# Splitting the expert weights, rows and inner values of two feed-forward stages into rounded high parts and rests

## The chip, the cores and the metric

The kernel runs on one core of one Trainium2 chip. The core has a matrix engine (PE, TensorE), whose weight loads are listed as PEld, a vector engine (DVE), a scalar engine (ACT), a general engine (POOL, GpSimd) and a queue of DMA instructions (SP). The metric is the device time of one execution in microseconds (us). Below, "pitch" is the distance between the starts of two neighbouring instructions of one kind.

## The reference, cut to what matters

A small network of eight stages in float32: an attention and a feed-forward stage in turn, each added to `x` after a normalisation. The change touches the feed-forward stages. The first two of them, called gated here, compute this on 1024 rows of 256 values:

```python
shared = _silu_and_mul(x @ shared_gate_up_w.T) @ shared_down_w.T      # inner width 704
shared = shared * jax.nn.sigmoid(x @ shared_gate_w.T)
probs = jax.nn.softmax(x @ gate_w.T, axis=-1)
routing_weights, selected_experts = jax.lax.top_k(probs, 2)           # 8 experts
for e in range(8):
    w_e = jnp.where(selected_experts == e, routing_weights, 0.0).sum(-1)
    h = _silu_and_mul(x @ w13[e].T) @ w2[e].T                         # inner width 176
    combined = combined + w_e[:, None] * h
out = shared + combined
```

The last two feed-forward stages (late) have the same experts' part, a smaller shared part (inner width 176) and no sigmoid.

## The kernel before, in words

One function, `ffn_stage`, writes each feed-forward stage as five programs, one for an engine, that run beside each other and wait for each other's semaphores. Within an engine the order is the order of the code. `early` is true in the two gated stages, where the shared part is cut in six pieces, four of them (`n_first`) ahead of the experts.

A gated stage runs in three parts. In the **front**, the 1024 rows are normalised and turned, the router's logits come out of PE, and DVE works out the routing in a chain of small instructions (lines 686 to 754): softmax, the two best experts of each row (`hit`), a rank from PE (`rank`, which waits for `hits_done`), and from it the lists `from_row` and `to_row` that say which rows make up each of 23 tiles of 128 rows (`rows_known`), and which expert owns a tile (`owner`). Meanwhile PE multiplies the first shared pieces: in its order stand `up(0, 0)`, `rank`, `up(0, 1)`, `up(1, 0)`, the list products, `up(1, 1)`, `clear_acc`, and `down(0)`, which waits for both `h_low(0, ...)` of DVE. ACT takes the gate products through `silu` and rounds `h` to a high part `h_hi`; DVE subtracts to get the rest `h_lo`. After `rows_known` PE has the rest of the first four pieces to do, and POOL starts eight gathers of 128 rows each (line 349).

In the **expert loop** each tile goes PE `turn_x` (L471, transpose of the gathered rows), ACT `x_out` (L610), PE `expert_up` (L484, two products of 128x352), ACT `silu_of` (L616) and DVE `h_of_tile` (L829), PE `turn_h` (L495), ACT `h_out` (L622), PE `expert_down` (L508, two products of 88x256), ACT `y_out` (L628), POOL `scatter` (L356). The tiles overlap: in PE's order `turn_x(i + 3)`, `expert_up(i + 2)`, `expert_down(i)` and `turn_h(i + 1)` follow each other. POOL alternates a scatter with a gather for the tile eight ahead (`XG_RING`), for 15 of the 23 tiles, and then only scatters. `y` has four buffers (`Y_RING`). These products take plain float32. The shared pieces use `product` (L78 to L80) instead: operands are split in a rounded high part and a rest of type fp32r, and high x high, rest x high and high x rest are added up.

In the **tail** the last two shared pieces and the scattered rows are added.

The eight experts' weights (128x1216 each, 608 KB) are loaded by SP in one go in the front and used as they come. POOL does nothing in the front between the store of the normalised rows and the first gather.

## Time and profile before

| | |
|---|---|
| median of 3 runs | 1727.43 us (1725.33 to 1733.93) |
| profiled execution, its own time | 1732.21 us |
| its span | 1730.4 us |
| busy: PE, DVE, ACT, POOL | 85%, 53%, 44%, 24% |
| granted PE clock, mean | 0.94 of full |

The profiled execution is one run with its own time; the span runs from its first instruction to its last. Line numbers are those of the kernel before. A "busy" share is an average over all eight stages. In the rows, one plain float32 product appears as two PE records, and names of tiles are written without their stage and number. A note in square brackets at the end of a row is how long the engine had been idle before it and what it waited for. In rows of a stretch, each engine has its busy time with the number of its instructions, then come the granted PE clock, the DMA share and GB/s.

### The profile page before, as it was taken

Reading aid. Unit: us, or ns where it says so; the run is one execution under the profiler, and the core shown is the slowest. Engines: PE = TensorE matmul, PEld = TensorE weight load, DVE = VectorE, ACT = ScalarE, POOL = GpSimd, SP = SyncE. Lnnn points to the kernel's source line nnn. Section 1 sums busy time; section 2 is a strip of 40 time slices with the busy share of each in tenths; the row PEclk is TensorE's granted clock in tenths of the full one; section 3 lists DMA queues with packets and bytes.
Section 4 is the critical chain, followed back from the end, with each engine's and each line's share of the span. In section 5 each row is a group of like instructions: output and inputs, shape, how many; then the busy total and the mean of one; then the engine's idle time right before and its main releaser. Section 6 shows DMA issues by size and latency. Waiting matters only on the chain. (4 is left out here: it accounts for less than half of the span.)

```text
span 1730.4 us, 27960 instructions
## 1 busy us (share of the span) xinstructions
PE 1476.0 (85%) x10106; PEld 1110.5 (64%) x10112; DVE 912.3 (53%) x1968; ACT 754.0 (44%) x1872; POOL 411.3 (24%) x328
## 2 busy tenths in 40 slices
PE   6999999995799789999899879878887787898587
PEld 4777787874576667767676657665555566533466
DVE  5766665663731846565555563176554314376712
ACT  5565656561334333433434434433443342586242
POOL 2607061210235221110201014520000451100162
PEclk9999999997899899999999989988897898899699
DMA  4002020100612400010000051230003223000423
GB/s 145 29 13 80 2 92 2 55 2 20 227 52 78 143 13 31 0 42 0 12 30 1 1 206 55 77 103 1 1 1 137 94 77 99 1 1 1 180 87 116
DMA packets 42996, 99.88 MB, mean 58 GB/s; under 512 B 7168, under 2 KB 21760, under 8 KB 42752
## 3 DMA queue, kind: packets, MB, share of 16 engines
q1 hardware_dynamic: 32736, 69.85, 11.8%
q0 software_dynamic: 9984, 28.32, 5.0%
q8 instruction: 76, 1.25, 0.3%
q14 instruction: 40, 0.33, 0.1%
q10 hardware_dynamic: 160, 0.13, 0.0%
HBM read 79.93 MB, written 18.35 MB: 57 GB/s over the span
## 5 line engine op out<-in xcount | busy, mean ns | idle before, releaser
L829 DVE TENSOR_TENSOR s_h_e<-s_bank,s_silu_e 128x176 f32<-128x176 f32 x92 | 31.4, 341 | 221.9 <-ACT s_silu_e L616 209.7
L484 PE MATMUL s_bank<-s_expert_w,s_xe 128*128 x368 | 130.5, 479 | 0.8 <-ACT s_xe L610 0.7
L508 PE MATMUL s_bank<-s_expert_w,s_he 88*128 x368 | 97.7, 387 | 30.6 <-ACT s_he L622 30.6
L356 POOL DMA_INDIRECT expert_rows<-s_y,s_to_row x92 | 91.3, 992 | 126.2 <-ACT s_y L628 114.3
L124 POOL TENSOR_SCALAR ln_var<-ln_moments 128x4 f32<-128x4 f32 x16 | 4.2, 260 | 492.3 <-DVE ln_moments L117 369.4
L349 POOL DMA_INDIRECT s_xg<-normed_rows,s_from_row x92 | 92.2, 1002 | 119.9 <-DVE s_from_row L744 93.1
L508 PEld LDWEIGHTS s_bank<-s_expert_w,s_he 88*128 88x128 f32 x368 | 68.4, 191 | 62.3 <-issue 43.7
L2555 POOL TENSOR_TENSOR s_w_hi<-s_w_raw,zero 128x1024 fp32r<-128x1024 f32 x25 | 55.3, 2213 | 220.6 <-PE s_memory L80 188.0
L1160 ACT ACTIVATE s_scratch<-s_bank,s_neg_max 128x128 f32<-128x128 f32 (+3 forms) x128 | 67.2, 528 | 89.2 <-DVE s_neg_max L1250 89.2
L1250 DVE TENSOR_REDUCE s_neg_max<-s_bank 128x1 f32<-128x128 f32 (+3 forms) x128 | 59.7, 488 | 74.2 <-PE s_bank L1063 74.1
L1080 PE MATMUL s_bank<-s_probs_t,s_v 128*128 128x512 f32 (+3 forms) x256 | 76.3, 441 | 20.2 <-ACT s_probs_t L1168 20.2
L1061 PE MATMUL s_bank<-s_k,s_q 128*128 128x128 f32 (+3 forms) x256 | 90.0, 447 | 3.0 <-ACT s_scratch L1160 2.2
L78 PE MATMUL s_bank<-xn_t_hi,s_w_hi 128*128 128x512 f32 x192 | 85.6, 446 | 7.8 <-DVE s_earlier L683 5.3
L981 POOL TENSOR_TENSOR s_w_hi<-s_w_raw,zero 128x1024 fp32r<-128x1024 f32 x11 | 22.3, 2026 | 272.1 <-PE s_bank L80 123.0
L2222 ACT ACTIVATE s_exps<-s_bank,s_rms 128x512 f32<-128x512 f32 x128 | 76.7, 696 | 21.3 <-PE s_bank L2108 21.3
L1080 PEld LDWEIGHTS s_bank<-s_probs_t,s_v 128*128 128x128 f32 x256 | 46.5, 190 | 55.0 <-ACT s_probs_t L1168 25.7
L484 PEld LDWEIGHTS s_bank<-s_expert_w,s_xe 128*128 128x128 f32 x368 | 65.3, 198 | 22.9 <-issue 4.3
L79 PE MATMUL s_bank<-xn_t_lo,s_w_hi 128*128 128x512 f32 x192 | 78.9, 411 | 0.0
L80 PE MATMUL s_bank<-xn_t_hi,s_w_lo 128*128 128x512 f32 x192 | 78.7, 410 | 0.0
L628 ACT ACTIVATE s_y<-s_bank 128x256 f32<-128x256 f32 x92 | 35.3, 384 | 94.0 <-PE s_bank L508 46.6
L1168 ACT ACTIVATE s_probs_t<-s_bank 128x128 f32<-128x128 f32 (+3 forms) x128 | 49.0, 437 | 59.9 <-PE s_bank L1074 59.9
L1260 DVE TENSOR_SCALAR s_scratch<-s_scratch,s_row_sum 128x128 f32<-128x128 f32 (+3 forms) x128 | 68.7, 537 | 4.5
(386 smaller groups left out, 4294.7 us busy)
## 6 DMA issues: line engine op xcount, KB each, us to landing
s_expert_w<-in_experts SPq DMA_DIRECT2D x32, 608.0 KB, 12.9
s_w_raw<-in_wa_o SPq DMA_DIRECT2D x16, 512.0 KB, 4.2
s_yg<-expert_rows SPq DMA_DIRECT2D x32, 256.0 KB, 4.6
s_raw<-in_shared SPq DMA_DIRECT2D x16, 384.0 KB, 6.9
normed_rows<-s_ln_xn POOLq DMA_DIRECT2D x8, 512.0 KB, 9.5
s_w_raw<-in_wa_k SPq DMA_DIRECT2D x4, 512.0 KB, 3.9
s_w_raw<-in_wa_v SPq DMA_DIRECT2D x4, 512.0 KB, 3.5
s_w_raw<-in_wa_q SPq DMA_DIRECT2D x4, 512.0 KB, 4.9
```

The source lines that it names most:

```text
L78: pe.matmul(out, sh, mh, start=first, stop=False, skip_group_check=True)
L79: pe.matmul(out, sh, ml, start=False, stop=False, skip_group_check=True)
L80: return pe.matmul(out, sl, mh, start=False, stop=last, skip_group_check=True)
L349: pool.indirect_dma_start(out=xg[:, i % XG_RING, :], out_offset=None, in_=x_rows[:, :], in_offset=bass.IndirectOffsetOnAxis(ap=from_row[:, ...
L356: pool.indirect_dma_start(out=y_rows[:, :], out_offset=bass.IndirectOffsetOnAxis(ap=to_row[:, i:i + 1].bitcast(U32), axis=0), in_=y[:, i % ...
L484: last = pe.matmul(u_bank[i % 2][:, 0:2 * INTER], xe[:, i % 2, x], expert_of(P, i, w), start=c == 0, stop=c == DC - 1, skip_group_check=True)
L508: last = pe.matmul(y_bank[i % 2][:, 0:D], he[0:IHALF, i % 2, h], expert_of(IHALF, i, w), start=c == 0, stop=c == 1, skip_group_check=True)
L1061: pe.matmul(to, q[:, b, h * S + r * P:h * S + (r + 1) * P], k[:, b, h, 0:(r + 1) * P], start=r == UNIT_ROWS[u][0], stop=False, skip_group_ ...
L1080: last = pe.matmul(o_bank[:, j * P:S], v[:, b, j, h * DH:(h + 1) * DH], probs_t[:, j, j * P:S], start=j == 0, stop=j == TB - 1, skip_group ...
L1160: act.activation(probs[:, h % 2, r, 0:(r + 1) * P], score_bank(h, r), ACT.Exp, bias=neg_max[:, 4 * h + r:4 * h + r + 1], accum_out=row_sum ...
L1260: dve.tensor_scalar(mine, mine, one, None, ALU.mult).then_inc(probs_done, 1)
L2222: act.activation(exps[:, s % 2, g, :], s_bank[g][:], ACT.Exp, scale=rms[:, b, 1, j:j + 1]).then_inc(exp_done, 1)
```

## The change

In the gated stages the experts' products are made like the shared ones, from split operands.

- Weights: `e_raw` holds three experts' raw weights (in the memory of `yg`, not needed until the tail). ACT rounds each expert to `e_hi` (128x1216, `expert_high`), and POOL subtracts to get `e_lo` (eight times, ahead of its waits for `x_stored` and `rows_known` and of the gathers). SP loads expert 3 and later ones into a slot when `e_lo` of the slot's last expert is done. ACT's eight copies stand at three places: three right after `gate_exp`, three after both `silu` of shared piece 0, two after those of piece 1.
- Rows and inner values: `x_out` and `h_out` write rounded tiles `xe_hi` and `he_hi`; DVE gets two more instructions for a tile, `x_low` (128x256) and `h_low_of_tile` (88x256), both PSUM tile minus SBUF tile.
- Products: three fp32r products in place of each plain one. PE waits for all eight `e_lo` ahead of the loop.
- `Y_RING` goes from 4 to 6, in all four feed-forward stages. The late stages have no other change.
- Memory: in the gated stages `silu` and `h_full` share memory with the normalised rows (so ACT waits for `x_stored` before its first `silu`), `logits_t` lies in `xg` and `slot_hit` in `y`.

```diff
-XG_RING, Y_RING = 8, 4
+XG_RING, Y_RING = 8, 6
+E_RING = 3
...
+            def expert_raw(one):
+                if one >= E_RING:
+                    sp.wait_ge(e_lo_done, one - E_RING + 1)
+                sp.dma_start(e_raw[:, one % E_RING, :], experts[one]).then_inc(e_raw_loaded[one % E_RING], 16)
...
                 sp.dma_start(raw[:, n % 3, :], shared[n]).then_inc(raw_loaded[n % 3], 16)
+                if early and n in (2, 3):
+                    for one in range(E_RING) if n == 2 else range(E_RING, N_EXP):
+                        expert_raw(one)
...
+            if early:
+                for one in range(N_EXP):
+                    pool.wait_ge(e_hi_done, one + 1)
+                    pool.tensor_tensor(e_lo[:, one, :], e_raw[:, one % E_RING, :], f32(e_hi[:, one, :]),
+                                       ALU.subtract).then_inc(e_lo_done, 1)
             pool.wait_ge(x_stored, 16 * NHALF)
             pool.wait_ge(rows_known, 1)
...
-                    last = pe.matmul(u_bank[i % 2][:, 0:2 * INTER], xe[:, i % 2, x], expert_of(P, i, w),
-                                     start=c == 0, stop=c == DC - 1, skip_group_check=True)
+                        last = product(pe, u_bank[i % 2][:, 0:2 * INTER], (xe_hi[:, i % 2, x], xe_lo[:, i % 2, x]),
+                                       (expert_of(e_hi, P, i, w), expert_of(e_lo, P, i, w)), c == 0, c == DC - 1)
...
+            def expert_high(one):
+                act.wait_ge(e_raw_loaded[one % E_RING], 16 * (one // E_RING) + 16)
+                act.activation(e_hi[:, one, :], e_raw[:, one % E_RING, :], ACT.Copy).then_inc(e_hi_done, 1)
+
+            if early:
+                for one in range(3):
+                    expert_high(one)
+                act.wait_ge(x_stored, 16 * NHALF)
...
                                        ACT.Silu).then_inc(silu_done, 1)
+                    if early and n < 2:
+                        for one in ((3, 4, 5), (6, 7))[n]:
+                            expert_high(one)
...
+            def x_low(i):
+                dve.wait_ge(xe_hi_done, i + 1)
+                if i >= 2:
+                    dve.wait_ge(u_ready, i - 1)
+                dve.tensor_tensor(xe_lo[:, i % 2, :], xt_bank[i % 2][:, 0:D], f32(xe_hi[:, i % 2, :]),
+                                  ALU.subtract).then_inc(xe_done, 1)
...
             if early:
-                for b in range(4):
-                    add_shared(b, 1)
-            for i in range(TILES):
-                h_of_tile(i)
+                add_shared(0, 1)
+                x_low(0)
+                x_low(1)
+                add_shared(1, 1)
+                add_shared(2, 1)
+                h_of_tile(0)
+                x_low(2)
+                add_shared(3, 1)
+                h_of_tile(1)
+                h_low_of_tile(0)
+                for i in range(TILES):
+                    if i + 3 < TILES:
+                        x_low(i + 3)
+                    if i + 2 < TILES:
+                        h_of_tile(i + 2)
+                    if i + 1 < TILES:
+                        h_low_of_tile(i + 1)
```

The order of POOL's instructions in the first gated stage (`s1`), around the store of the normalised rows, before:

```order
L127 TENSOR_TENSOR ln_rstd<-ln_var,ln_power 128x4
L343 DMA normed_rows<-s1_ln_xn 128x4x256 x2
L349 DMA s1_xg<-normed_rows,s1_from_row 128x256 x8
L356 DMA expert_rows<-s1_y,s1_to_row 4992x256
L349 DMA s1_xg<-normed_rows,s1_from_row 128x256
```

and now (`s1_yg` holds the raw weights):

```order
L128 TENSOR_TENSOR ln_rstd<-ln_var,ln_power 128x4
L367 DMA normed_rows<-s1_work 128x4x256 x2
L387 TENSOR_TENSOR s1_expert_lo<-s1_yg,s1_expert_hi 128x1216 x8
L373 DMA s1_xg<-normed_rows,s1_from_row 128x256 x8
L380 DMA expert_rows<-s1_y,s1_to_row 4992x256
```

Eight subtractions now stand between the store and the first gather; the rest of the order is the same.

ACT's order in the same stage from `gate_exp` on, before:

```order
L585 ACTIVATE s1_gate_exp<-s1_logits 128x8
L593 ACT_TABLE_LOAD
L593 ACTIVATE s1_silu<-s1_bank4 128x512
L593 ACTIVATE s1_silu<-s1_bank6 128x512
L599 ACTIVATE s1_h_hi<-s1_h_full 128x512 x2
L593 ACTIVATE s1_silu<-s1_bank4 128x512
L593 ACTIVATE s1_silu<-s1_bank6 128x512
L599 ACTIVATE s1_h_hi<-s1_h_full 128x512 x2
L570 ACTIVATE s1_w_hi<-s1_raw 128x768
```

and now (`s1_work` holds `silu` and `h_full`):

```order
L625 ACTIVATE s1_gate_exp<-s1_logits 128x8
L629 ACTIVATE s1_expert_hi<-s1_yg 128x1216 x3
L642 ACT_TABLE_LOAD
L642 ACTIVATE s1_work<-s1_bank4 128x512
L642 ACTIVATE s1_work<-s1_bank6 128x512
L629 ACTIVATE s1_expert_hi<-s1_yg 128x1216 x3
L651 ACTIVATE s1_h_hi<-s1_work 128x512 x2
L642 ACTIVATE s1_work<-s1_bank4 128x512
L642 ACTIVATE s1_work<-s1_bank6 128x512
L629 ACTIVATE s1_expert_hi<-s1_yg 128x1216 x2
L651 ACTIVATE s1_h_hi<-s1_work 128x512 x2
```

Three copies came ahead of the first `silu`, three ahead of the two roundings of `h` for piece 0, and two ahead of those for piece 1.

PE's order for one tile of the expert loop, from `turn_x` over `find_owner` (the load and two register instructions) to the first product of `expert_up`, before:

```order
L471 MATMUL s1_bank7<-ident,s1_xg 128x128 x2
L515 TENSOR_LOAD s1_owner
L515 ISA x2
L484 ISA
L484 MATMUL s1_bank5<-s1_expert_w,s1_xe 128x352
```

and now, over the same stretch:

```order
L500 MATMUL s1_bank7<-ident,s1_xg 128x128 x2
L552 TENSOR_LOAD s1_owner
L552 ISA x2
L79 ISA
L79 MATMUL s1_bank5<-s1_expert_hi,s1_xe_hi 128x352
L80 REGISTER_ALU
L80 MATMUL s1_bank5<-s1_expert_lo,s1_xe_hi 128x352
L81 MATMUL s1_bank5<-s1_expert_hi,s1_xe_lo 128x352
```

Where one plain product stood with one register instruction ahead, three rounded ones stand with two. The same holds for the second product of `expert_up` and for both of `expert_down`.

## Rows read from the trace of the kernel before

**Rows 1.** Windows: PE, PEld, DVE, ACT, POOL busy us (instructions), clock, DMA share, GB/s.
```profile
452.00:468.40 16.40, 14.31 (x74) 10.92 (x76) 13.12 (x61) 4.97 (x9) 0.00 (x0) 0.90 0.60 243
468.40:491.50 23.10, 23.10 (x148) 20.74 (x148) 12.81 (x24) 8.47 (x13) 8.71 (x8) 1.00 0.16 46
```

**Rows 2.** Timeline of ACT, front of the first gated stage (start, duration, work, idle before).
```profile
452.83 0.20 ACT L585 ACTIVATE s_gate_exp<-s_logits 128x8 f32<-128x8 f32 x1
458.52 0.60 ACT L593 ACTIVATE s_silu<-s_bank 128x512 f32<-128x512 f32 x1 [3.58 <-PE s_bank L80]
```

**Rows 3.** Timeline of DVE, same stretch: routing chain.
```profile
456.32 0.22 DVE L706 TENSOR_TENSOR s_hits<-s_hit 128x64 bf16<-128x64 f32 x1
461.54 2.36 DVE L732 TENSOR_TENSOR s_slot_hit<-s_routing,s_in_slot 128x1024 bf16<-128x1024 f32 x2
467.90 0.18 DVE L744 TENSOR_SCALAR s_from_row<-s_to_row 128x23 int32<-128x23 int32 x1
```

**Rows 4.** Timeline of POOL and DVE in the second attention stage.
```profile
649.33 1.89 POOL L981 TENSOR_TENSOR s_w_hi<-s_w_raw,zero 128x1024 fp32r<-128x1024 f32 x1 [31.68 <-DMA s_w_raw<-in_wb_k]
649.48 1.90 DVE L1260 TENSOR_SCALAR s_scratch<-s_scratch,s_row_sum 128x256 f32<-128x256 f32 x1
651.30 2.38 POOL L984 TENSOR_TENSOR s_w_lo<-s_w_raw,s_w_hi 128x1024 fp32r<-128x1024 f32 x1
651.48 2.42 DVE L1260 TENSOR_SCALAR s_scratch<-s_scratch,s_row_sum 128x384 f32<-128x384 f32 x1
```

**Rows 5.** Timeline of POOL and DVE in the first attention stage.
```profile
59.58 2.41 POOL L2558 TENSOR_TENSOR s_w_lo<-s_w_raw,s_w_hi 128x1024 fp32r<-128x1024 f32 x1
59.81 2.72 DVE L2915 SCALAR_TENSOR_TENSOR s_sigma_qt<-s_exp_part,s_positive 128x512 f32<-128x512 f32 x1 [1.46 <-ACT s_positive L2820]
```

**Rows 6.** Timeline of POOL and DVE, second attention stage, an earlier place.
```profile
597.49 3.34 POOL L981 TENSOR_TENSOR s_w_hi<-s_w_raw,zero 128x1024 fp32r<-128x1024 f32 x1 [11.23 <-DMA s_w_raw<-in_wb_v]
598.99 1.87 DVE L1227 TENSOR_SCALAR s_bq<-s_bq 128x16 f32<-128x16 f32 x1
```

**Rows 7.** Line 2558: the POOL subtraction of two SBUF tiles (min/median/max ns).
```profile
L2558 POOL TENSOR_TENSOR s_w_lo<-s_w_raw,s_w_hi x25: 2355/2407/2730, 39.8 to 352.0; 128x1024 fp32r<-128x1024 f32 x25
```

**Rows 8.** Line 570: an ACT copy that rounds SBUF to SBUF.
```profile
L570 ACT ACTIVATE s_w_hi<-s_raw x16: 833/842/864, 446.0 to 1621.0; 128x768 fp32r<-128x768 f32 x16
```

**Rows 9.** The page's part 6: a weight load (KB each, us to landing).
```profile
s_w_raw<-in_wa_o SPq DMA_DIRECT2D x16, 512.0 KB, 4.2
```

**Rows 10.** Timeline of PE: rounded products of 256 columns.
```profile
470.07 0.28 PE L78 MATMUL s_bank<-s_w_hi,s_h_hi 128*128 128x256 f32 x1
470.19 0.28 PE L79 MATMUL s_bank<-s_w_lo,s_h_hi 128*128 128x256 f32 x1
```

**Rows 11.** Timeline of PE in the expert loop: the two transposes of a tile.
```profile
509.19 0.38 PE L495 MATMUL s_bank<-ident,s_h_e 128*88 128x128 f32 x2
509.41 0.38 PE L471 MATMUL s_bank<-ident,s_xg 128*128 128x128 f32 x2
```

**Rows 12.** Timeline of ACT, line 628 alone: the copies y_out of the expert loop.
```profile
498.08 0.39 ACT L628 ACTIVATE s_y<-s_bank 128x256 f32<-128x256 f32 x1 [0.55 <-PE s_bank L508]
500.57 0.38 ACT L628 ACTIVATE s_y<-s_bank 128x256 f32<-128x256 f32 x1 [0.55 <-PE s_bank L508]
507.44 0.38 ACT L628 ACTIVATE s_y<-s_bank 128x256 f32<-128x256 f32 x1 [1.88 <-remote]
559.77 0.38 ACT L628 ACTIVATE s_y<-s_bank 128x256 f32<-128x256 f32 x1 [1.30 <-PE s_bank L508]
```

**Rows 13.** Timeline of POOL in that loop: a scatter.
```profile
510.67 1.00 POOL L356 DMA_INDIRECT expert_rows<-s_y,s_to_row  x1 [0.30 <-issue]
```

**Rows 14.** Line 628: what ended one kind of its waits (us, times).
```profile
  remote: 42.0, 17
```

**Rows 15.** Windows around an idle PE ahead of a late feed-forward stage.
```profile
1320.00:1325.50 5.50, 0.06 (x1) 0.06 (x1) 4.30 (x14) 0.00 (x0) 1.34 (x2) 0.50 0.09 26
1328.00:1331.00 3.00, 2.26 (x9) 1.70 (x8) 2.94 (x7) 2.59 (x5) 0.09 (x1) 0.50 0.90 307
```

More of the change, by code:

```diff
@@ L226, in ffn_stage @@
         xt_bank, u_bank, ht_bank, y_bank = (banks[4], banks[7]), banks[5:7], banks[0:2], banks[2:4]
-        norm = Norm(nc, ctx, sem, f"{name}_ln", res, [b[:] for b in banks[4:8]], measured=measured)
+        work = sb("work", [P, 2 * NHALF, HALF])
+        silu, h_full = work[:, 0:NHALF, :], work[:, NHALF:2 * NHALF, :]
+        norm = Norm(nc, ctx, sem, f"{name}_ln", res, [b[:] for b in banks[4:8]], measured=measured,
+                    xn=work[:].rearrange("p a (b d) -> p (a b) d", d=D) if early else None)
         following = Moments(sem, "next_ln", res)
@@ L231, in ffn_stage @@
         w_hi, w_lo = sb("w_hi", [P, 3, SH_COLS], F32R), sb("w_lo", [P, 3, SH_COLS], F32R)
-        e = sb("expert_w", [P, N_EXP, EXP_COLS])
+        yg = sb("yg", [P, TOP_K, NT, D])
+        y = sb("y", [P, Y_RING, D])
+        if early:
+            e_hi, e_lo = sb("expert_hi", [P, N_EXP, EXP_COLS], F32R), sb("expert_lo", [P, N_EXP, EXP_COLS], F32R)
+            e_raw = yg[:].rearrange("p k t d -> p (k t d)")[:, 0:E_RING * EXP_COLS].rearrange("p (r n) -> p r n", r=E_RING)
+        else:
+            e = sb("expert_w", [P, N_EXP, EXP_COLS])
         tables = sb("routing", [P, TABLE_COLS])
@@ L291, in ffn_stage @@
         xt_ready, xe_done, e_loaded = sem("xt_ready"), sem("xe_done"), sem("expert_w_loaded")
+        e_raw_loaded = [sem(f"expert_raw_loaded{r}") for r in range(E_RING)]
+        e_hi_done, e_lo_done = sem("expert_hi_done"), sem("expert_lo_done")
+        xe_hi_done, he_hi_done = sem("xe_hi_done"), sem("he_hi_done")
         u_ready, silu_e_done, h_e_done = sem("u_ready"), sem("silu_e_done"), sem("h_e_done")
@@ L507, in expert_down @@
                     w = slice(EXP_DOWN + c * D, EXP_DOWN + (c + 1) * D)
-                    last = pe.matmul(y_bank[i % 2][:, 0:D], he[0:IHALF, i % 2, h], expert_of(IHALF, i, w),
-                                     start=c == 0, stop=c == 1, skip_group_check=True)
+                    if early:
+                        last = product(pe, y_bank[i % 2][:, 0:D], (he_hi[0:IHALF, i % 2, h], he_lo[0:IHALF, i % 2, h]),
+                                       (expert_of(e_hi, IHALF, i, w), expert_of(e_lo, IHALF, i, w)), c == 0, c == 1)
+                    else:
+                        last = pe.matmul(y_bank[i % 2][:, 0:D], he[0:IHALF, i % 2, h], expert_of(e, IHALF, i, w),
+                                         start=c == 0, stop=c == 1, skip_group_check=True)
                 last.then_inc(y_ready, 1)
```

48 lines of the change are left out of this document (35 added, 13 removed).

## The prediction

> **What bounds the kernel now.** I read the page first, then the busy time of the engines in windows of a gated stage, then the timelines of the engines in them, and last two places elsewhere where POOL does what it is now to do in the front.
>
> In the front of the first gated stage PE is busy 14.31 of 16.40 us and DVE 13.12, while POOL has not one instruction [rows 1]. After it comes a stretch of 23.10 us in which PE has no gap at all [rows 1]. So whatever moves the end of the front moves everything behind it by as much; and that end is the end of DVE's routing chain. It runs without a break from the hits at 456.32 over the slot comparison at 461.54 to `from_row`, which ends at 468.08 [rows 3]. The second gated stage has the same code and sizes; I give it the same.
>
> In the expert loop two tiles without a stall are 2.49 us apart, yet the 22 intervals from 498.08 to 559.77 take 61.69 us where 22 x 2.49 would be 54.8 [rows 12]. The rest are stalls: the first three tiles take 9.36 us instead of 7.47, and the wait that ends it is given as "remote" [rows 12], which stands for 17 waits and 42.0 us over all four feed-forward stages [rows 14].
>
> **The loop: products.** Per tile, four plain products become twelve rounded ones. The rounded product of 256 columns has a pitch of 0.12 us [rows 10]. The trace has none of 352 columns; in proportion to the columns it takes 0.162. Six of 0.162 and six of 0.118 are 1.68 us, and the two pairs of transposes keep 0.22 each [rows 11]: 2.12 us of PE work in place of 2.49. That is the lower end of the new period. The upper end is the old 2.49: the path from `turn_h` over `h_out` to `expert_down` gets one more instruction, `h_low_of_tile`, and PE's queue has twice the register instructions for a tile. I take 2.30, the middle.
>
> The Trainium skill ("TensorE: Matmul & The Clock Gate", Back-to-back issue gap and the section on 56 ns ahead of it) gives an isolated matmul of N columns N/2.4 + 2.5 ns; for 352 that is 149 ns and for 256 it is 109. The trace is 8% above that at 256 columns. By the page the PE work would be 1.99 us a tile and not 2.12; what the runs show per tile decides.
>
> **The loop: stalls.** They are no lack of `y` buffers. The copy that stalls at 507.44 is that of tile 3 (498.08, 500.57, one more, then this), the first use of the fourth buffer, which waits for no store at all [rows 12]. What it waits for is PE's signal, which arrives late while POOL is issuing a gather. So the ring of six cures nothing by itself, and the two late stages, which get only that, stay as they are (0 us; bound: rival C). In the gated stages the stalls depend on how PE's signals fall against POOL's issues. POOL needs 1.30 us for a scatter [rows 13] and as much for a gather, 2.6 a tile for the first 15 tiles, so at a period of 2.30 the two drift apart and a signal meets an issue now and then. I take three stalls of 1.9 us (from 9.36 - 7.47), with none and seven as ends. Loop: 22 x 2.30 + 5.7 = 56.3, that is -5.4 us a stage; -11.1 without stalls, about -1 with a period near 2.4 and all stalls kept. POOL's 15 x 2.6 + 8 x 1.3 = 49 us stay below that.
>
> Between front and loop DVE has to make two or three `x_low` ahead of the first up product: +0.3 us.
>
> **The front: ACT.** Eight copies of 128x1216. A rounding copy of 128x768 takes 0.84 us [rows 8]; in proportion to the columns less some fixed part I estimate 1.22, or 9.8 us in all. ACT has 4.97 of 16.40 us busy there [rows 1], so its time is there; its order is what costs. The first three end at 456.7 and hold back the first `silu`, which had nothing but a table load ahead of it; its result is needed by `h_of(0, 0)`, which costs the chain up to 2. Experts 3 to 5 can only be loaded when `e_lo` of 0 to 2 is done: with 2.86 us each for those (below) the last is done at 462.9, a load takes some 4.3 us (512 KB take 4.2 [rows 9]), the copy 1.2, so `h_hi` of piece 0, which stands behind it in ACT's order, comes at 468.4 and not right behind the `silu` of 458.52 [rows 2]. `h_low(0, 0)` stands in DVE's order ahead of the last six routing instructions. That alone puts `rows_known` at 471.2 in place of 468.1: **+3.1 us**.
>
> **The front: POOL beside DVE.** This is the main term. The subtraction on POOL takes 2.36 to 2.73 us for 128x1024 [rows 7]; for 128x1216 I estimate 2.86 from the median 2.41, and eight are 23 us. While such an instruction runs, certain DVE instructions do not get through: a 128x256 multiplication by a scalar takes 1.90 us and ends 0.16 after POOL's; the next one takes 2.42 and again ends 0.22 after POOL's next, which had slipped in between [rows 4]. The 128x512 one with two SBUF inputs takes 2.72 and ends 0.55 after POOL's [rows 5], and even one of 128x16 takes 1.87 and ends with it [rows 6]. So with POOL's instructions back to back, DVE gets one such instruction done per POOL instruction.
>
> The routing chain is made of these: comparisons, products and casts of SBUF tiles. Walking both queues forward: `e_hi(0)` is done at 454.3 (`gate_exp` ends at 453.03 [rows 2] plus 1.2), POOL runs `e_lo(0)`, (1), (2) until 463.5 with handovers of 0.2. DVE reaches its cast of the indices 0.6 ahead of the hits, at 455.7, gets it done at 457.3, the first comparison at 460.2, the second and the sum `hits` at 463.7 instead of 456.54: +7.2. PE's `rank` waits for it, and behind `rank` PE's gate product for `silu(0, 1)`, which was ready at 458.52 [rows 2], 2.0 after the hits; ACT's next copies stand behind that `silu`. So POOL pauses until about 468, DVE runs free for that time up to the tile comparisons, and then `e_lo(3)`, (4) and (5) each hold one of the large comparisons or the `h_low`: three more blocks of 2.6 to 2.9, 8.2 us. Then ACT's queue needs `h_of(0, 1)`, POOL is idle and the rest runs free. Sum +15.4 a stage, `rows_known` at 483.5; the 3.1 us of ACT's order lie inside it. Low end: if casts and scalar instructions on integers do not block, 13.1. High end: four blocks in the second group, 18.4. `e_lo(6)` and (7) and the gathers follow under the 23.1 us of PE work and cost nothing; were that cover gone, 5.7 us.
>
> The Trainium skill ("SBUF — State Buffer", Who interferes with whom) says that a DVE instruction with two SBUF inputs contends with a GpSimd instruction that reads SBUF, that copies, casts and `tensor_scalar` contend only in a two-port mode, that reductions never do, and that whoever issues first holds the shared ports for the whole instruction. The trace agrees on the first, with 2.72 us of which 0.55 lay behind POOL's end, and shows a scalar instruction of 128x16 blocked too (1.87 us, where one of 128x23 in the chain takes 0.18 [rows 3]). If the small casts are not in that mode, the front would be the low end, 13.1.
>
> **The clock.** PE will wait some 10 us in the front. After an idle stretch of 5.50 us elsewhere it is still granted half speed (0.50, 1.2 GHz) in a window 2.5 to 5.5 us later [rows 15]. If the first 3 to 7 us of the 23.10 run at half speed, that costs half of them; I take 2.0, ends 0 and 3.3.
>
> **Sum.** Per gated stage +15.4 + 2.0 + 0.3 - 5.4 = +12.3, rounded to 12; two are +24. The profiled execution took 1732.21 us and would take 1756; it lies 4.8 above the median of its runs, 1727.43, and the forecast on that is 1751. Own range: low 13.1 + 0 + 0.3 - 11.1 = +2.3 a stage (1732), high 18.4 + 3.3 + 0.3 - 1 = +21 (1769).
>
> **Rivals.** A: the front is not blocked. The rows on blocking are of instructions on large tiles or alone in a queue, and the chain has other semaphores between its steps, which might let several instructions through at each handover. Then a stage costs +3.1 + 0.3 - 5.4 = -2.0, total 1723; with no stalls 22 x 2.30 gives -7.7, total 1712. The point from which it decides: the front and the clock together must grow by under 9.4 us a stage for the whole to stay within 8.6 us of before. For it speaks nothing in the trace that I found; against it, rows 4 to 6. C: the ring of six is what the "remote" waits wanted. Then all 17 go, 1.9 us each: -32 over four stages; with the blocked front 1727 + 2 x (15.4 + 2.0 + 0.3 - 11.1) - 17 of the late stages = about 1724, and without it near 1696. Against it speaks the stall on the fourth buffer. D: the loop gains nothing (the chain over `h_low_of_tile` or PE's queue keeps 2.49 and the stalls stay): 2 x 17.7 = +35, 1762.
>
> **Chances.** What a measurement of this kernel can tell from no change is about 0.5%, 8.6 us. Forecast 0.72 (slower 0.64, same 0.08); A 0.15 (same 0.08, faster 0.07); C 0.06 (half same, half faster); D 0.07 (slower). Together slower 0.71, same 0.19, faster 0.10. The range takes the forecast's own and reaches down into A: 1721 to 1769.
>
> **What would show it.** In the profile after: long DVE times (1 to 3 us) on lines of the routing chain that took 0.2, each ending with a POOL subtraction; POOL subtractions of about 2.9 us; `rows_known` some 15 us later against the stage's start; the stretch of unbroken PE work still 23 us or a little over. In the loop, product pitches of 0.16 and 0.12, tiles 2.3 us apart, some waits called "remote" left; the late stages unchanged to the tenth of a us. A front that grows by 3 us or less would make the main term wrong; remote waits gone from the late stages would make the reading of the ring wrong; a loop period of 2.49 would leave no gain at all.

## The result, and the profile after

The changed kernel takes 1769.09 us (median of 4 runs, 1764.86 to 1781.26), the one before 1728.35 (4 runs, 1725.33 to 1733.93): a ratio of 1.025, 95% interval 1.0219 to 1.0281. The profiled execution after took 1766.43 us with a span of 1764.6. The forecast was 1751 with a range to 1769. The time lies 0.09 us outside that edge, which decides nothing by itself (the sum behind it, 1727.43 + 2 x 21, is 1769.4); what has to be explained is that the loss of 41 us is 1.7 times the 24 forecast.

The two spans differ by 34.2 us. Read off the timelines (row maximum of the logits, `rows_known`, first and last `y_out` of each stage), in us:

| stretch | before | after | forecast |
|---|---|---|---|
| row maximum to `rows_known`, gated 1 and 2 | 15.92, 15.90 | 31.64, 31.66 | +15.4 each |
| `rows_known` to `y_out(0)`, gated 1 and 2 | 30.01, 30.04 | 32.53, 31.84 | +2.3 each |
| loop, gated 1 and 2 | 61.69, 62.00 | 64.03, 64.19 | -5.4 each |
| loop, late 1 and 2 | 62.11, 62.20 | 60.56, 60.72 | 0 |
| all the rest (difference) | | -3.1 | 0 |

The windows that answer to [rows 1]: the front, the stretch right after `rows_known`, and the rest of the PE work. Columns as there.

```profile
452.00:483.00 31.00, 14.84 (x74) 10.63 (x72) 30.17 (x54) 12.48 (x14) 24.64 (x9) 0.78 0.38 127
482.00:485.00 3.00, 3.00 (x12) 2.33 (x11) 2.80 (x8) 1.01 (x2) 2.17 (x2) 0.50 0.15 44
485.00:488.00 3.00, 3.00 (x18) 3.00 (x17) 0.95 (x2) 0.22 (x1) 2.18 (x3) 0.57 0.32 87
488.00:506.00 18.00, 18.00 (x108) 15.89 (x108) 7.31 (x11) 7.24 (x11) 3.52 (x4) 1.00 0.13 38
```

POOL, idle in the front before, is busy 24.64 of 31.00 us, DVE shows 30.17 and PE 14.84. The granted PE clock is half (0.50, 1.2 GHz) behind `rows_known`, still 0.57 on average from 485 to 488, and full (1.00, 2.4 GHz) afterwards.

The same stretch on POOL's and DVE's timelines; it answers to [rows 3]. First two rows of before that are not there, then the rows after:

```profile
455.92 0.36 DVE L704 TENSOR_TENSOR s_hit<-iota,s_at_f 128x64 f32<-128x64 f32 x2
...
467.46 0.18 DVE L742 TENSOR_TENSOR s_row<-s_row,s_spare 128x23 f32<-128x23 f32 x1
```

```profile
452.00 8.20 POOL L387 TENSOR_TENSOR s_expert_lo<-s_yg,s_expert_hi 128x1216 fp32r<-128x1216 f32 x3 [9.61 <-ACT s_expert_hi L629]
465.67 15.87 POOL L387 TENSOR_TENSOR s_expert_lo<-s_yg,s_expert_hi 128x1216 fp32r<-128x1216 f32 x5 [5.48 <-ACT s_expert_hi L629]
```

```profile
453.49 1.33 DVE L756 CAST s_at_f<-s_at 128x16 f32<-128x16 uint32 x1
454.86 5.42 DVE L758 TENSOR_TENSOR s_hit<-iota,s_at_f 128x64 f32<-128x64 f32 x2
460.31 0.23 DVE L760 TENSOR_TENSOR s_hits<-s_hit 128x64 bf16<-128x64 f32 x1
...
465.33 4.99 DVE L786 TENSOR_TENSOR s_y<-s_routing,s_in_slot 128x1024 bf16<-128x1024 f32 x2
...
470.25 0.68 DVE L718 TENSOR_TENSOR s_work<-s_bank,s_work 128x512 f32<-128x512 f32 x1
470.85 2.67 DVE L725 TENSOR_TENSOR s_h_lo<-s_work,s_h_hi 128x512 fp32r<-128x512 f32 x1
...
473.65 0.18 DVE L794 TENSOR_TENSOR s_row<-s_row,s_bank 128x23 f32<-128x23 f32 x1
...
474.08 2.08 DVE L796 TENSOR_TENSOR s_row<-s_row,s_spare 128x23 f32<-128x23 f32 x1
476.20 2.68 DVE L797 SCALAR_TENSOR_TENSOR s_to_row<-s_row,s_routing 128x23 int32<-128x23 f32 x1
478.91 2.66 DVE L798 TENSOR_SCALAR s_from_row<-s_to_row 128x23 int32<-128x23 int32 x1
```

The two comparisons of `hit` took 5.42 us where they took 0.36, the cast ahead of them 1.33 where a cast took 0.17, the two of `slot_hit` 4.99 against 2.36, and three instructions of 128x23 took 2.08, 2.68 and 2.66 against 0.18 each. Between 460.2 and 465.7 POOL paused, and there the chain runs at its old pace. Two kinds of DVE instruction were not held while POOL ran: the index searches, and those that take one of two inputs from PSUM (`s_bank`), 0.68 us at 470.25 and 0.18 us at 473.65 as before. The subtraction itself, and the copies ACT makes for it:

```profile
L387 POOL TENSOR_TENSOR s_expert_lo<-s_yg,s_expert_hi x16: 2732/2772/3782, 452.0 to 1070.8; 128x1216 fp32r<-128x1216 f32 x16
```

```profile
L629 ACT ACTIVATE s_expert_hi<-s_yg x16: 1200/1210/1217, 450.7 to 1068.7; 128x1216 fp32r<-128x1216 f32 x16
```

In the loop, the `y_out` rows that answer to [rows 12], and the sum that answers to [rows 14]:

```profile
514.10 0.38 ACT L682 ACTIVATE s_y<-s_bank 128x256 f32<-128x256 f32 x1 [0.38 <-PE s_bank L81]
...
516.39 0.38 ACT L682 ACTIVATE s_y<-s_bank 128x256 f32<-128x256 f32 x1 [0.40 <-PE s_bank L81]
...
520.49 0.38 ACT L682 ACTIVATE s_y<-s_bank 128x256 f32<-128x256 f32 x1 [1.87 <-remote]
...
522.74 0.38 ACT L682 ACTIVATE s_y<-s_bank 128x256 f32<-128x256 f32 x1 [1.12 <-PE s_bank L81]
...
526.86 0.38 ACT L682 ACTIVATE s_y<-s_bank 128x256 f32<-128x256 f32 x1 [1.89 <-remote]
```

```profile
  remote: 30.4, 15
```

Between two stalls a tile takes 2.25 to 2.29 us (forecast 2.30), but in the first two thirds of the loop about every second one stalls and takes 4.1: seven such tiles in each gated loop against five before. The profile calls ten of these fourteen waits remote, as it does seven of the ten before; the others it puts down to PE or names no releaser for. In 13 of the fourteen the copy starts 0.80 to 0.93 us behind the end of a gather; here is the one ahead of the copy at 520.49:

```profile
518.66 0.97 POOL L373 DMA_INDIRECT s_xg<-normed_rows,s_from_row  x1 [0.31 <-issue]
```

A gather being issued is not enough for a stall, though: the copy at 516.39 started inside one (516.07 to 517.05).

The products of PE in that loop, answering to [rows 10]:

```profile
530.06 0.32 PE L81 MATMUL s_bank<-s_expert_hi,s_xe_lo 128*128 x1
530.22 0.32 PE L79 MATMUL s_bank<-s_expert_hi,s_xe_hi 128*128 x1
...
530.70 0.28 PE L79 MATMUL s_bank<-s_expert_hi,s_he_hi 88*128 x1
530.83 0.28 PE L80 MATMUL s_bank<-s_expert_lo,s_he_hi 88*128 x1
```

Their pitch is 0.16 us for 352 columns and 0.12 to 0.13 for 256, as forecast.

### The profile page after: what moved, and what is told of

The parts are those of the page before. It is cut to its first block and busy times, and to the rows that moved or that the text cites. A ratio compares the mean times of both kernels' runs of the same rounds, so it can differ in the third digit from the quotient of the medians.

```text
span 1764.6 us, 28724 instructions
## 1 busy us (share of the span) xinstructions
PE 1478.1 (84%) x10296; PEld 1126.6 (64%) x10296; DVE 982.6 (56%) x2060; ACT 772.3 (44%) x1888; POOL 458.1 (26%) x344
## 5 line engine op out<-in xcount | busy, mean ns | idle before, releaser
L373 POOL DMA_INDIRECT s_xg<-normed_rows,s_from_row x92 | 90.8, 987 | 70.0 <-DVE s_from_row L798 43.2
L1878 DVE TENSOR_REDUCE s_neg_max<-s_pair 128x2 f32<-128x1024 f32 (+3 forms) x64 | 51.7, 823 | 36.3 <-PE s_pair L1656 35.5
L2999 DVE SCALAR_TENSOR_TENSOR s_sigma_qt<-s_exp_part,s_positive 128x512 f32<-128x512 f32 x32 | 50.5, 1584 | 29.9 <-ACT s_positive L2904 29.8
L517 PE MATMUL s_bank<-s_expert_w,s_xe 128*128 x184 | 64.8, 476 | 0.0
L2642 POOL TENSOR_TENSOR s_w_lo<-s_w_raw,s_w_hi 128x1024 fp32r<-128x1024 f32 x25 | 63.4, 2537 | 2.0
## 6 DMA issues: line engine op xcount, KB each, us to landing
s_expert_w<-in_experts SPq DMA_DIRECT2D x16, 608.0 KB, 11.7
```

Source lines behind the costliest of these rows:

```text
L373: pool.indirect_dma_start(out=xg[:, i % XG_RING, :], out_offset=None, in_=x_rows[:, :], in_offset=bass.IndirectOffsetOnAxis(ap=from_row[:, ...
L517: last = pe.matmul(u_bank[i % 2][:, 0:2 * INTER], xe[:, i % 2, x], expert_of(e, P, i, w), start=c == 0, stop=c == DC - 1, skip_group_check ...
L2642: pool.tensor_tensor(w_lo[:, slot, :], w_raw[:, slot, :], f32(w_hi[:, slot, :]), ALU.subtract).then_inc(w_split[slot], 1)
```

## The experiments

Four sets, each on one chip and with runs of the kernel before among them. In the first set the kernel before took 1697.5 us, in the others 1726.1, 1730.9 and 1736.6. The difference goes with the remote waits: in the loops of the first set no trace has one (the kernel before has no trace of its own there, but e1_ring6 took the same 1697.5 us). So the sets are compared within themselves, by ratio, and by stretches. "Front" is row maximum to `rows_known`, "lead" is `rows_known` to `y_out(0)`, both of the gated stages. "Theory" and "rival" in the expectations are two explanations that the run is to tell apart.

**First set, without remote waits.** The ring of six alone:

```diff
-XG_RING, Y_RING = 8, 4
+XG_RING, Y_RING = 8, 6
```

> The kernel before with Y_RING 6 in place of 4 and nothing else. Theory (the remote waits are PE's signals held up while POOL issues a gather, no lack of y buffers): about as many remote waits as before (17), the gated loops still 61 to 62 us; 1724 to 1729 us, the late loops perhaps 1.5 us shorter each, as in the changed kernel (60.6 in place of 62.1). Rival (the ring is what the waits wanted): the 17 waits of some 1.9 us go, about 1696 us.

Ratio 1.0008 (0.9987 to 1.003). There was nothing to cure, so this run says only that the ring neither costs nor gives anything by itself; it was repeated below.

The subtraction in eight pieces:

```diff
-                    pool.tensor_tensor(e_lo[:, one, :], e_raw[:, one % E_RING, :], f32(e_hi[:, one, :]),
-                                       ALU.subtract).then_inc(e_lo_done, 1)
+                    for piece in range(8):
+                        at = slice(piece * EXP_COLS // 8, (piece + 1) * EXP_COLS // 8)
+                        last = pool.tensor_tensor(e_lo[:, one, at], e_raw[:, one % E_RING, at], f32(e_hi[:, one, at]),
+                                                  ALU.subtract)
+                    last.then_inc(e_lo_done, 1)
```

> The changed kernel, with each POOL subtraction of an expert's weights cut into eight instructions of 152 columns; the work and its place in the order are the same. Theory (a POOL instruction holds DVE's second port from its start to its end, and DVE gets one turn between two): each blocked DVE instruction now waits 0.4 us at most instead of 2.8; from the row maximum of the logits to rows_known 19 to 22 us in place of 31.6 (before: 15.9), in total 20 to 25 us less than the changed kernel, 1744 to 1749. Rival (the front is late for another cause: ACT's order, the loads in three slots): under 5 us less, 1764 or more.

The front is 23.0 us in place of 31.6 (the theory's 19 to 22 was a little low, since a piece takes longer than an eighth). The total can't be set against the changed kernel of another occasion; against the kernel before it is 1.0105 (1.006 to 1.0149). POOL's pieces and some DVE rows of that front:

```profile
L389 POOL TENSOR_TENSOR s_expert_lo<-s_yg,s_expert_hi x128: 494/511/1487, 451.7 to 1059.0; 128x152 fp32r<-128x152 f32 x128
```

```profile
453.66 0.95 DVE L761 TENSOR_TENSOR s_hit<-iota,s_at_f 128x64 f32<-128x64 f32 x2
...
471.29 0.43 DVE L799 TENSOR_TENSOR s_row<-s_row,s_spare 128x23 f32<-128x23 f32 x1
...
472.22 0.42 DVE L801 TENSOR_SCALAR s_from_row<-s_to_row 128x23 int32<-128x23 int32 x1
```

The blocked time follows the length of POOL's instruction: 0.43 us where whole subtractions made it 2.08 to 2.68. ACT's order and the loads were not touched, so the rival falls as the main cause; 7.1 us of front are left. By stretches the change costs 2 x (7.1 + 1.3 - 1.1) = 15 us here (front, lead, loop), and the medians differ by 16.3. The loops, without stalls, are 52.3 and 52.6 us against 53.5 (the products of before, in e3_ahead): the rounded products gain 1.1 us a stage and no more, since tiles alternate between 2.25 and 2.45 us, and the three last tiles, which took 1.95 to 2.3 before, do not get shorter.

A memset in place of the subtraction (`pool.memset(e_lo[:, one, :].bitcast(F32), 0.0)`):

> The changed kernel with a POOL memset to zero of the experts' low parts in place of the subtraction: it leaves the low parts of the expert weights out. The instruction reads nothing from SBUF and writes the same bytes. Theory (a POOL instruction that reads SBUF holds the port): DVE instructions with two SBUF inputs run unhindered; from the row maximum of the logits to rows_known 16 to 20 us in place of 31.6. Rival (any long POOL instruction blocks DVE): DVE instructions on the chain still take the length of the memset, each ending with one.

The front is 19.0 and 20.5 us (one run). POOL's memsets and DVE's rows beside them:

```profile
453.99 3.32 POOL L387 MEMSET s_expert_lo<- 128x1216 f32 x3 [9.58 <-ACT s_expert_hi L628]
460.63 1.11 POOL L387 MEMSET s_expert_lo<- 128x1216 f32 x1 [3.33 <-ACT s_expert_hi L628]
```

```profile
455.51 0.72 DVE L755 CAST s_at_f<-s_at 128x16 f32<-128x16 uint32 x1
456.27 0.36 DVE L757 TENSOR_TENSOR s_hit<-iota,s_at_f 128x64 f32<-128x64 f32 x2
456.66 0.23 DVE L759 TENSOR_TENSOR s_hits<-s_hit 128x64 bf16<-128x64 f32 x1
458.08 0.69 DVE L717 TENSOR_TENSOR s_work<-s_bank,s_work 128x512 f32<-128x512 f32 x1 [1.20 <-ACT s_work L641]
...
460.78 0.99 DVE L775 CAST s_in_tile_int<-s_position 128x16 int32<-128x16 f32 x1
```

The comparisons with two SBUF inputs (456.27) run at their old 0.36 us beside a memset, where a subtraction made them 5.42. The casts are still held, each until the memset beside it ends: 0.72 and 0.99 in place of 0.17. So both theories hold a part: two SBUF inputs were held only by a POOL instruction that reads SBUF, casts by one that only writes as well. "SBUF — State Buffer" of the Trainium skill (Who interferes with whom) draws that line too, and gives for the casts a mode with two ports; the rows agree with the line, and no run here shows the mode. Of the 3.1 us that the front still costs in this stage, 1.0 is ACT's order (DVE waits 1.20 us at 458.08 for a `silu` behind the three copies, 0.20 before), and the rest is held casts and scalar instructions.

All 23 gathers of a gated stage ahead of its loop:

```diff
-            for i in range(XG_RING):
+            for i in range(ahead):
                 gather(i)
...
+        ahead = TILES if early else XG_RING
+            return spare_xg[:, i - XG_RING, :] if early and i >= XG_RING else xg[:, i % XG_RING, :]
...
-                    out=xg[:, i % XG_RING, :], out_offset=None, in_=x_rows[:, :],
+                    out=x_slot(i), out_offset=None, in_=x_rows[:, :],
```

`spare_xg` is the memory of `yg`, and every tile has a semaphore of its own.

> The kernel before, with all 23 gathers of a gated stage issued ahead of its loop (tiles 8 to 22 into the memory of yg, which is unused until the tail); POOL only scatters in the loop. Theory (the stall needs a gather issued in the loop): no remote waits in the two gated loops, each 54 to 55 us in place of 61.7 to 62.0, the late stages the same; 1712 to 1715 us. Rival (scatters hold up PE's signals as well, or the stalls have nothing to do with POOL): loops of 60 us or more, 1724 to 1729.

Ratio 1.0005 (0.9984 to 1.0026), all loops 53.49 us: nothing to see without remote waits, so neither theory nor rival was tested.

**Second set, with remote waits.** The changed kernel again:

> The changed kernel once more, beside the kernel before on one chip. In the four kernels of the first set there was not one remote wait in any loop and the kernel before took 1697.5 us, 31 less than in its first runs. Theory (remote waits depend on the chip, not on the kernel; the change costs its front everywhere): without remote waits, front +15.7, from rows_known to y_out(0) +2, loop -1.2 a gated stage: 33 us above the kernel before, 1731; with remote waits, 40 above it and every loop like the first runs. Rival (the change owes its cost to the stalls alone): without remote waits within 10 us of the kernel before.

Ratio 1.0248 (1.0207 to 1.0289), 1771.74 us against 1726.14, fronts 31.64 and 31.67, gated loops 63.96 and 63.98, late ones 60.7 and 61.1. The change costs the same again. The waits were back, on the same chip that had shown none in the first set, so they do not come with the chip alone, as this theory had it, and the rival was not tested. The changed kernel was not run on an occasion without them. From stretches of other runs its cost there would be 2 x (15.7 + 2 - 1.1) = 33 us, an estimate; a comparison in the fourth set gives more (below).

The changed kernel with all gathers ahead (the edit of e3_ahead, behind a wait for the last subtraction):

> The changed kernel, with all 23 gathers of a gated stage issued between the subtractions and the loop (tiles 8 to 22 into the memory of yg). If this chip shows remote waits: theory (they need a gather issued in the loop) none in the gated loops, 52 us each in place of 64; rival (scatters do it too) loops of 60 or more. If it shows none: as e4_again within 3 us.

The gated loops are 53.1 and 52.1 us, the late ones, not edited, 60.9: without a gather in the loop there is no remote wait in it. But the lead grew from 31.3 and 32.2 to 47.3 and 48.3 us. That is not POOL's time: its last gather ended at 512.79 and `y_out(0)`, which needs tile 0 alone, came at 530.45. The waits moved ahead of the loop:

```profile
516.58 0.84 ACT L618 ACTIVATE s_w_hi<-s_raw 128x768 fp32r<-128x768 f32 x1 [19.73 <-remote]
```

```profile
511.60 0.59 PE L81 MATMUL s_bank<-xn_t_hi,s_w_lo 128*128 128x512 f32 x1 [1.52 <-issue]
```

ACT stood for 19.73 us, and PE itself was held: from 500 to 510 it started ten products and was busy 4.96 us. Ratio 1.0275 (1.0221 to 1.0329), so it gives nothing.

The subtractions behind `rows_known`:

```diff
-            if early:
-                for one in range(N_EXP):
-                    pool.wait_ge(e_hi_done, one + 1)
...
+                    if early and n < n_first:
+                        for one in ((0, 1, 2), (3,), (5, 7))[n - 1]:
+                            dve.wait_ge(e_hi_done, one + 1)
+                            dve.tensor_tensor(e_lo[:, one, :], e_raw[:, one % E_RING, :], f32(e_hi[:, one, :]),
+                                              ALU.subtract).then_inc(e_lo_done[one], 1)
```

The second part stands in DVE's run over the shared pieces, behind the `h_low` of pieces 1 to 3; POOL keeps experts 4 and 6, behind its first eight gathers.

> The changed kernel with the subtractions out of the front: DVE does six of them and POOL two (experts 4 and 6, behind the first eight gathers), all after rows_known, under the 23 us of PE work; ACT's first three copies stand between the two silu of piece 0, the others behind the roundings of pieces 2 and 3. Theory (the front is paid for by POOL and DVE sharing a port in the routing chain): from the row maximum to rows_known 16 to 17 us, from there to y_out(0) 31 to 33.5, loops as in e4_again; within 6 us of the kernel before. Rival (the eight copies and loads cost as much wherever they stand): 15 us or more above the kernel before.

The fronts are 16.2 and 16.1 us: the 15.7 us are gone, and no work was removed from the kernel. (ACT's copies and most loads moved too, so this run alone does not say which of them the front had paid for; e2_cut8 and e5_memset left copies and their places alone.) The lead is 40.2 and 40.3, because the work now ends too late. Ratio 1.0159 (1.0115 to 1.0204), 1755 against 1772 of the changed kernel in the same set. The rows of ACT and DVE at its end:

```profile
489.84 0.84 ACT L615 ACTIVATE s_w_hi<-s_raw 128x768 fp32r<-128x768 f32 x1 [4.23 <-PE s_bank L81]
490.59 2.31 ACT L634 ACTIVATE s_expert_hi<-s_yg 128x1216 fp32r<-128x1216 f32 x2
```

```profile
490.72 0.96 DVE L716 TENSOR_TENSOR s_w_lo<-s_raw,s_w_hi 128x768 fp32r<-128x768 f32 x1 [4.37 <-ACT s_w_hi L615]
491.59 5.30 DVE L832 TENSOR_TENSOR s_expert_lo<-s_yg,s_expert_hi 128x1216 fp32r<-128x1216 f32 x2
```

The last two roundings stood behind ACT's `w_hi` (489.84), which waits for PE's last down product, and then DVE's second subtraction met POOL's, which ran from 491.87 to 495.61, and was held once more: 5.30 us for two.

And with `find_owner` moved:

```diff
                 if i + 3 < TILES:
+                    find_owner(i + 3)
                     turn_x(i + 3)
                 if i + 2 < TILES:
-                    find_owner(i + 2)
                     expert_up(i + 2)
```

> As e8_late, with the read of a tile's owner (a register load on PE's queue) moved ahead of the transposes of the same step, one tile earlier. Where e2_cut8's tiles alternate between 2.25 and 2.45 us, PE is idle 0.2 us behind the transposes until the first up product can be dispatched. Theory (the queue's register work makes that gap): periods of 2.1 to 2.3 us, gated loops 47 to 50 us in place of 52.3, 5 to 9 us less than e8_late. Rival (the chain over DVE's two more instructions sets the period): no change.

Ratio 1.0172 (1.0126 to 1.0219), loops 63.8 against 63.8 and 62.9 in e8_late, and the last periods still alternate between 2.25 and 2.45 to 2.7. The register load of a tile's owner is not what makes the second 0.2 us; what does stays open.

**Third set, with remote waits.** All subtractions on DVE, three behind `h_low` of piece 1, three of piece 2, two of piece 3:

```diff
-        by_pool = (4, 6)
+        by_pool = ()
...
-                        for one in ((0, 1, 2), (3,), (5, 7))[n - 1]:
+                        for one in ((0, 1, 2), (3, 4, 5), (6, 7))[n - 1]:
```

> As e8_late, but DVE does all eight subtractions, and ACT's and DVE's work on experts 3 to 7 stands ahead of that on the next shared piece's weights. In e8_late the last rounding copies stood behind PE's last down product and the loop began 10 us late. Theory (with the split under the PE work of the four pieces the change costs nothing in the front): from rows_known to y_out(0) 31 to 33 us in place of 40.2, 14 to 17 us less than e8_late; without remote waits within 5 us of the kernel before, with them 5 to 10 above. Rival (what is left is the work itself, wherever it stands): 36 us or more.

Lead 34.6 and 34.4 us (the theory said 31 to 33, the rival 36 or more: between them), fronts 15.9 and 16.2, ratio 1.0081 (1.0047 to 1.0116). Two thirds of the change's cost (13 us are left of 41 to 46) are gone by placing the same work elsewhere. What is left is 4.5 us of lead and 2 to 3 us of loop a stage.

The ring of six again:

> The kernel of e1_ring6 again, for the same reason. With remote waits about, theory: the ring of six leaves them, loops 60.5 to 62.2, at most 6 us under the kernel before. Rival (the ring cures them): loops of 53.5, 32 us less.

Ratio 0.9998 (0.9979 to 1.0016), 12 remote waits left, loops 60.6 to 62.3. The ring of six shortens some loops by up to 1.5 us and cures nothing; rival C falls. The late loops of the changed kernel moved by the same 1.5.

The kernel before with the gathers ahead again:

> The kernel of e3_ahead again (kernel before, 23 gathers of a gated stage ahead of its loop), since its first runs fell on an occasion without remote waits. With remote waits about, theory (a gather issued in the loop is needed for one): gated loops 53.5 in place of 61.7 to 62.0, late ones 62.1; 16 us under the kernel before. Rival: gated loops of 60 or more, no gain. Without them: no difference, once more.

The gated loops are 53.49 us as the theory said, but the kernel is slower: 1.0078 (1.0051 to 1.0105). The lead grew from 30 to 43.2 and 44.9 us. PE's chain waits there instead; these are DVE's row at the end of that wait and POOL's last gather:

```profile
485.80 0.69 DVE L670 TENSOR_TENSOR s_h_full<-s_bank,s_silu 128x512 f32<-128x512 f32 x1 [2.51 <-PE s_bank L80]
497.02 0.69 DVE L670 TENSOR_TENSOR s_h_full<-s_bank,s_silu 128x512 f32<-128x512 f32 x1 [10.53 <-remote]
```

```profile
497.04 0.95 POOL L355 DMA_INDIRECT s_yg<-normed_rows,s_from_row  x1 [0.30 <-issue]
```

DVE waited 10.53 us, "remote", for a product that PE had finished, and went on as POOL came to its last gather. In the first set the same kernel's lead was 30.0. My theory was half right: the waits need gathers, but taking them out of the loop moves the price: the loops gained 8 us each and the leads lost 13 and 15.

The same in all four stages (`ahead = TILES`, `Y_RING` 8):

> As e3b_ahead, in all four feed-forward stages and with eight y buffers: in the late stages the gathers take 29 us, 16 of them beside the first tiles, and the first scatter waits for them. With remote waits about, theory: late loops with stalls in the first 16 us only, 56 to 58 us in place of 62.1, so 8 to 12 us under e3b_ahead. Rival (gathers back to back stall each of those tiles): late loops of 62 or more. Without remote waits the late loops stay at 53.5 or grow by 1 to 3 for the late scatters.

Late loops of 74.7 us, ratio 1.0219: gathers back to back hold the first tiles for 9 and 14 us. The rival holds.

**Fourth set, with remote waits: what they hang on.** In place of the gather for tiles 8 to 22:

```diff
                 if i >= XG_RING:
                     pool.wait_ge(xt_ready, i - XG_RING + 1)
+                    pool.dma_start(xg[:, i % XG_RING, :], x_rows[(i % XG_RING) * P:(i % XG_RING + 1) * P, :]).then_inc(xg_loaded[i % XG_RING], 16)
+                    return
```

> The kernel before, with the gathers for tiles 8 to 22 replaced by plain loads of 128 rows that POOL issues at the same places (it leaves the choice of the rows out). With remote waits about, theory (the indirect gather holds PE's signals up): loops of 53.5 to 55 us in all four stages, 30 us under the kernel before. Rival (any load that POOL issues does): loops of 60 or more.

Ratio 0.9799 (0.9746 to 0.9852). All four loops are 53.49 us, with POOL issuing a load for each tile:

```profile
519.98 1.00 POOL L358 DMA_INDIRECT expert_rows<-s_y,s_to_row  x1 [0.92 <-ACT s_y L630]
520.99 0.56 POOL L349 DMA_DIRECT2D s_xg<-normed_rows  x1
522.47 1.00 POOL L358 DMA_INDIRECT expert_rows<-s_y,s_to_row  x1 [0.93 <-ACT s_y L630]
```

```profile
521.81 0.38 ACT L630 ACTIVATE s_y<-s_bank 128x256 f32<-128x256 f32 x1 [0.55 <-PE s_bank L510]
...
524.30 0.38 ACT L630 ACTIVATE s_y<-s_bank 128x256 f32<-128x256 f32 x1 [0.55 <-PE s_bank L510]
```

Tiles of 2.49 us and no remote wait: it is the indirect gather, not a load from POOL's queue and not the scatter, which is still there and still indirect. (Two runs; that the waits were about in this set is shown by e2b_cut8 below.)

The same loads from SP's queue:

> As e12_direct, with the plain loads issued by SP, so that POOL only scatters in the loop (the choice of the rows is left out here too). Both theories: loops of 53.5 us, 30 us under the kernel before. If the waits stay, they hang on the scatters or on the traffic itself, and POOL's queue has no part in it.

Ratio 0.9766 (0.9715 to 0.9817), loops 53.49: the same, as both theories said.

The changed kernel without the lines `if i + XG_RING < TILES: gather(i + XG_RING)`:

> The changed kernel without any load of rows in the loop: tiles 8 to 22 work on what lies in the eight buffers (their rows are left out). Theory: no remote waits, gated loops of 51.5 to 52.6 us, late ones 53.5, so 35 to 40 us under the changed kernel, 1733 to 1738 where that takes 1771. Rival (scatters hold PE's signals up as well): gated loops of 58 or more.

Gated loops 52.8 and 52.7, late 53.49, 1737.05 us, as much as the kernel before with its waits (1736.6). Against e4_again by stretches, the loops of all four stages are 37 us shorter. This is also the nearest thing to the change's cost without the waits: 37 us above e12_direct and 43 above e13_sp_loads, which are kernels of before without indirect gathers in the loop (two runs each). The stretches of the gated stages give 34 of them.

The subtraction in eight pieces again:

> The kernel of e2_cut8 again (subtractions in eight pieces), whose first runs fell on an occasion without remote waits. With them about: from the row maximum to rows_known 23.0 us as there, gated loops 63.5 to 64.5 as in the changed kernel, 12 to 19 us under the changed kernel and 25 to 30 above the kernel before (1.015 to 1.018); without them 1.0105 once more.

Fronts 22.6 and 23.5, gated loops a little over the range at 64.8 and 64.7, ratio 1.0168 (1.0113 to 1.0222), as the theory said. The leads were not: 36.5 and 33.4 us, where e2_cut8 has 31.5 and 31.1. In the first of them stands this row:

```profile
483.56 6.84 DVE L728 TENSOR_TENSOR s_h_lo<-s_work,s_h_hi 128x512 fp32r<-128x512 f32 x2 [3.90 <-ACT s_h_hi L654]
```

The first of the two took 6.24 us and ended 0.55 behind the last of a run of POOL's pieces, 12 of which began and ended meanwhile. So a turn for DVE between two POOL instructions is what nearly all rows show, but it is not assured.

No kernel that computes everything beat the one before.

## Why the prediction was wrong, point by point

- **The front, POOL beside DVE: right, in mechanism and size.** +15.7 and +15.8 us against +15.4. e2_cut8, e5_memset and e8_late show the cause from three sides: the block follows the length of POOL's instruction, its kind, and its place. That the size fits to 0.4 us is in part luck. `hits` moved by 6.2 us (460.31 + 2.2 for the earlier start of the stage, against 456.32; forecast 7.2), and POOL paused behind `silu(0, 1)` as walked. But the second group was taken as three blocks of 8.2 us, with POOL idle afterwards and `e_lo(6)` and `(7)` free of cost behind `rows_known`. In the trace the five subtractions left ran back to back until 481.54, five DVE instructions were held (the second `slot_hit`, one `h_lo`, the last three of the chain), and the group cost 9.5. The low end of 13.1 had casts and scalar instructions run free; they are held (1.33 and 2.66 us). The 3.1 us of ACT's order alone were never seen: e5_memset shows 1.0.
- **Clock and transition: right.** +2.5 and +1.8 us against +2.3 (e4_again: +1.3 and +2.1).
- **The loop's period: half right.** A tile without a wait takes 2.25 to 2.29 us between two waits against 2.30; but where no wait falls it alternates with 2.45, and 22 intervals take 52.3 us and not 50.6. Before, they take 53.5 without waits and not 54.8, since the last ones are shorter. The products alone gain 1.1 us a stage, where the term had 4.2.
- **The loop's stalls: wrong, and this is most of the miss.** The step was "I take three stalls of 1.9 us, with none and seven as ends", to which belonged "about -1 with a period near 2.4 and all stalls kept". Their size was about right (4.10 - 2.27 = 1.83; over the whole loop 64.0 - 52.3 us for seven, 1.7 each); seven came, and where the stalls of before were kept as the worst case (five, by the intervals), there were more of them. The range did not even use its own end of seven: 22 x 2.30 + 7 x 1.9 = 63.9 is +2.2 a stage, where its high side took -1 (and that sum, 22 x 2.4 and the 6.9 us of stalls before, gives -2). With +2.2 the upper bound would have been 1776. That 63.9 is close to the 64.0 measured is luck, a period too short and stalls too long. A gated loop came out at 64.0 us against 56.3: 1.7 by the period and 6 by the stalls, which makes +2.3 and +2.2 instead of -5.4, or 15.3 us over both stages. I argued that signals and issues would drift apart at the new period, and did not walk it. The rows spoke against it: 2.6 us of POOL for a tile [rows 13] are more than a period of 2.30, so POOL would hardly pause in the first 15 tiles and most signals would meet an issue. What makes some of them wait and others not is not known. With the stalls as forecast the time would have been about 1757.
- **The sum.** In the profiled pair (34.2 us) these 15.3 us are partly given back by the rest (-3.1) and the late loops (-3.0); the medians, four runs each, differ by 40.7, against 24.6 forecast. The 6.5 us between the two lie within what runs of one kernel spread here (16.4 us between the lowest and the highest of the four after).
- **The ring: right.** It gives at most 1.5 us a stage (e1b_ring6), and the stall is not a lack of buffers.
- **The late stages** were forecast unchanged and their loops were 1.5 us shorter each. e1b_ring6 points to that ring, but e2b_cut8, with a ring of six too, has late loops of 61.8 and 62.2.
- **Rivals.** A, the unblocked front, and C, the ring as cure, fell. D was nearest in the end: it had the loop gain nothing and gave 1762, 7 us short. Its mechanism did not come about, though: the period did fall below 2.49, and added stalls took back more than that.

## What to carry to other kernels

Before work is given to an idle POOL, list what DVE does in that stretch: beside POOL instructions that read SBUF, back to back, DVE got about one comparison, product, cast or scalar instruction on SBUF tiles done per POOL instruction, however small it was. Put such work beside DVE instructions with an input in PSUM, which were not held (0.68 and 0.18 us), or cut it in pieces; a chain of tiny instructions on SBUF is the worst neighbour of all. Where a wait in the old trace recurs at some beat that hangs on the phase of two engines, a change of the period can raise its count, here from five to seven. Take a wait on every turn as the bound, not the old count.

## What the runs showed that I had not expected

- The same kernel took 1697.5 us on one occasion and 1726 to 1737 on others. The remote waits account for it: 17 in the trace of before [rows 14] and none in the traces of the first set, and the four loops together take 248.0 and 214.0 us (e3_ahead's 53.49 each). The first two sets, 1697.5 and 1726.1 us, ran on the same chip.
- They hang on the indirect gather alone (e12_direct). For 15 gathers a stage they cost 8.2 us in the loop of before, 11.7 in that of the changed kernel (64.0 against 52.3), and 13 to 16 ahead of the loop (e3b_ahead, e6_after_ahead). The scatters, indirect as well and 23 a stage, cost nothing of the kind, and neither did the first eight gathers of the kernel before, whose lead is 30.0 us with or without the waits. Why some occasions have them and others not was not found.
